# A graph layer and a routed expert layer on one core: four neighbouring tokens to a partition for x and the output, chunk 0 loaded behind x's first group, and the first chunks' projections one group ahead

## What is computed

```python
def reference(x, adj, ...):
    # graph layer, on the layer-normalised x
    h = layernorm(x)
    filt = tanh(adj * adj) * (adj > 0)
    new_adj = filt, with the 350 largest entries of each row kept
    h2 = tanh(h @ W_proj + b_proj)
    x = x + relu(new_adj @ (h2 @ W_gcn) + b_gcn)
    # expert layer, on the layer-normalised x
    t = layernorm(x)
    gate = t @ Wg.T + bg                  # (4096, 8)
    s, idx = top_k(gate, 2); p = softmax(s)
    for e in range(8):
        y = relu(t @ W1[e].T + b1[e]) @ W2[e].T + b2[e]
        x = x + combine[:, e] * y         # combine: p where e is in idx
    return x
```

## Time and profile before

| | us |
|---|---|
| median of 3 runs | 454.85 |
| lowest and highest | 454.68, 456.05 |
| profiled execution, its own time | 453.6 |
| its span, first to last instruction | 451.8 |
| PE busy | 399.7 (88%) |
| ACT busy | 329.6 (73%) |
| DVE busy | 324.6 (72%) |
| POOL busy | 201.3 (45%) |
| mean granted TensorE clock | 0.966 |

### The profile page before, as it was taken

One profiled execution on the slowest core, in us unless ns is written; L12 is line 12 of the kernel. 1 busy time (PEld: TensorE's weight loads), 2 busy tenths in 40 slices (PEclk: granted clock), 3 DMA queues, 4 the chain that ended last, 5 costly groups with the idle time before them and its releaser, 6 DMA issues.

```text
span 451.8 us, 7828 instructions
## 1 busy us (share of the span) xinstructions
PE 399.7 (88%) x2392; PEld 231.9 (51%) x2392; DVE 324.6 (72%) x946; ACT 329.6 (73%) x329; POOL 201.3 (45%) x296
## 2 busy tenths in 40 slices
PE   1799999999899899999999999999697999999600
PEld 1555434344344344444454544446596889999500
DVE  5977887562997898765849776964988766676435
ACT  2788999679989879979989989953454666666300
POOL 5048976000005303512610846623657777777700
PEclk9999999999999999999999999999898999999955
DMA  8828997866378676866873979924533464531069
GB/s 248 324 96 295 411 400 258 303 232 247 107 265 309 205 270 217 306 259 220 311 284 107 319 224 319 301 41 80 95 73 119 115 114 106 103 88 59 22 243 318
DMA packets 54260, 95.01 MB, mean 210 GB/s; under 512 B 34037, under 2 KB 41258, under 8 KB 46018
## 3 DMA queue, kind: packets, MB, share of 16 engines
q1 hardware_dynamic: 43584, 79.40, 52.9%
q0 software_dynamic: 5920, 12.78, 8.8%
q10 hardware_dynamic: 4706, 2.23, 1.7%
HBM read 77.90 MB, written 12.27 MB: 200 GB/s over the span
## 4 chain that ended last, share of the span: by engine, by line
PE 64%; DVE 18%; issue 5%; ACT 4%; DMA 4%; POOL 1%; ACTq 1%; SPq 1%; POOLq 0%; DVEq 0%
PE bank L1453 35%; PE bank L1581 6%; PE bank L1468 3%; PE bank L1555 3%; ACT tbuf L1193 3%; PE bank L1582 3%; PE bank L1557 3%; PE bank L1556 3%; DMA tbuf<-expert_rows 2%; PE bank L1424 2%; DVE stats L745 1%; PE bank L1408 1%; DVE tbuf L1100 1%; PE bank L1540 1%; DVE aug L738 1%
## 5 line engine op out<-in xcount | busy, mean ns | idle before, releaser
L1453 PE MATMUL bank<-tbuf,g_sb 128*128 128x512 f32 x512 | 234.4, 602 | 0.3 <-ACT tbuf L1197 0.3
L1453 PEld LDWEIGHTS bank<-tbuf,g_sb 128*128 128x128 f32 x512 | 93.0, 192 | 101.1 <-issue 99.8
L1193 ACT ACTIVATE tbuf<-abuf 128x2048 f32<-128x2048 f32 x64 | 121.5, 1898 | 7.8 <-DVE key L1077 4.2
L1197 ACT ACTIVATE tbuf<-tbuf 128x2048 f32<-128x2048 f32 x64 | 122.3, 1911 | 2.0
L691 POOL DMA_INDIRECT routed_rows<-aug,slots x64 | 74.0, 1157 | 102.9 <-DVE base L904 83.5
L705 POOL DMA_INDIRECT expert_rows<-abuf,xmeta x72 | 70.9, 985 | 27.2 <-issue 16.5
L918 DVE TENSOR_SCALAR marks<-abuf 128x2048 bf16<-128x2048 int32 x64 | 80.4, 1265 | 2.0 <-PE bank L1468 1.9
L1581 PE MATMUL bank<-w2hl,tbuf 128*128 x288 | 53.5, 279 | 5.8 <-DVE tbuf L1100 5.8
L1582 PE MATMUL bank<-w2hl,tbuf 128*128 x288 | 51.6, 224 | 0.0
L1100 DVE SCALAR_TENSOR_TENSOR tbuf<-bank,tbuf 128x512 f16<-128x512 f32 x72 | 46.7, 685 | 5.8 <-ACT tbuf L1294 5.3
L1302 ACT ACTIVATE abuf<-bank,xmeta 128x128 f32<-128x128 f32 x72 | 23.0, 365 | 38.2 <-PE bank L1582 38.2
(11 more groups left out here) (246 smaller groups left out, 420.5 us busy)
## 6 DMA issues: line engine op xcount, KB each, us to landing
abuf<-in_adj_tiles SPq DMA_DIRECT2D x64, 1024.0 KB, 5.7
wstage<-in_w POOLq DMA_DIRECT2D x16, 256.0 KB, 7.1
tbuf<-expert_rows SPq DMA_DIRECT2D x8, 512.0 KB, 7.2
out<-xres ACTq DMA_DIRECT2D x8, 256.0 KB, 6.3
routed_rows<-pad SPq DMA_DIRECT2D x9, 130.0 KB
expert_rows<-abuf,xmeta POOLq DMA_INDIRECT x72, 2.4
routed_rows<-aug,slots POOLq DMA_INDIRECT x64
abuf<-routed_rows SPq DMA_TRANSPOSE x40
```

The lines of the kernel that those rows point to most:

```text
L1193: act.activation(tbuf[:, n % NBUF, :, :], abuf[:, n % NBUF, :, :], ACT.Square).then_inc(s_sq, 1)
L1197: act.activation(tbuf[:, n % NBUF, :, :], tbuf[:, n % NBUF, :, :], ACT.Tanh).then_inc(s_t, 1)
L1453: last = pe.matmul(ps_feat[ib % 2][:, :], g_sb[:, c, :], tbuf[:, buf, cc, :], start=(c == 0), stop=(c == C - 1))
```

## The change

Six things change; line numbers are those of before.

1. `xres` holds four neighbouring tokens in each partition: group g, partition p and column group c now hold token g*512 + 4p + c. `load_x` and the output store read and write 2048 contiguous bytes for each partition and group where they had four runs of 512.
2. The transposed normalised x comes out of PE in the order (c, p). `turned_out` writes it to `xnorm_t` in the order (p, c), a step of four elements (16 bytes) between neighbouring elements of its write. From there the projections read as before, and `g_sb`, the adjacency and the counts keep their order.
3. `features_back` reads its stationary operand from `feat_t` with a step of four elements (16 bytes), where it read 128 contiguous columns.
4. SP issues x piece 0, chunk 0, x piece 1, chunk 1, x piece 2, chunk 2, where it issued x piece 0, x piece 1, chunk 0, x piece 2, chunk 1.
5. PE transposes group 1 in the middle of chunk 0, and projects group n + 1 in the middle of chunk n for n of 1 and more; it transposes group n + 2 behind chunk n. ACT follows in the same order, and squares chunk 0 ahead of the first transposed group.
6. All steps of WAT lie one later.

```diff
-    WAT = [1 + i for i in range(2 * NPC)]
+    WAT = [2 + i for i in range(2 * NPC)]
...
-                sp.dma_start(xres[:, c0:c1, :], x[c0 * P:c1 * P, :].rearrange("(c p) d -> p c d", p=P)
-                             ).then_inc(s_x[i], 16)
+                sp.dma_start(xres[:, c0:c1, :].rearrange("p (g c) d -> p g c d", c=CK),
+                             x[c0 * P:c1 * P, :].rearrange("(g p c) d -> p g c d", p=P, c=CK)).then_inc(s_x[i], 16)
 
             load_x(0)
-            load_x(1)
             for n in range(NCH):
...
                 sp.dma_start(abuf[:, n % NBUF, :, :], adj_tiles[n // NK, n % NK, :, :, :]).then_inc(s_a[n % NBUF], 16)
-                if n == 0:
-                    load_x(2)
+                if n < 2:
+                    load_x(n + 1)
...
                 act.wait_ge(s_tr, g + 1)
-                act.activation(xnorm_t[:, g * IW:(g + 1) * IW], [ps_x2, ps_xn][g % 2][:, :], ACT.Copy
+                act.activation(xnorm_t[:, g * IW:(g + 1) * IW].rearrange("d (p c) -> d c p", c=CK),
+                               [ps_x2, ps_xn][g % 2][:, :].rearrange("d (c p) -> d c p", c=CK), ACT.Copy
                                ).then_inc(s_trc, 1)
...
+            square_chunk(0)
             turned_out(0)
-            square_chunk(0)
+            tanh_chunk(0)
             projected_out(0)
-            tanh_chunk(0)
-            turned_out(1)
...
                     square_chunk(n + 1)
+                    if n == 0:
+                        turned_out(1)
                     tanh_chunk(n + 1)
-                if n == 0:
-                    projected_out(1)
-                    turned_out(2)
+                if n + 1 < NK:
+                    projected_out(n + 1)
                 if n + 2 < NK:
-                    projected_out(n + 2)
-                if n + 3 < NK:
-                    turned_out(n + 3)
+                    turned_out(n + 2)
...
-                act.dma_start(out[g * IW:(g + 1) * IW, :].rearrange("(c p) d -> p c d", p=P),
+                act.dma_start(out[g * IW:(g + 1) * IW, :].rearrange("(p c) d -> p c d", p=P),
...
             project(0)
-            turn_group(1)
...
                 for cc in range(SUB):
-                    c = b * SUB + cc
-                    last = pe.matmul(x2[:, cc * D:(cc + 1) * D], feat_t[:, c * P:(c + 1) * P], wg_sb[:, :],
+                    last = pe.matmul(x2[:, cc * D:(cc + 1) * D], feat_t[:, b * IW + cc:(b + 1) * IW:SUB], wg_sb[:, :],
...
                 for cc in range(CK):
+                    if n + 1 < NK and cc == CK // 2:
+                        project(n + 1) if n else turn_group(1)
...
                 if n == 0:
                     project(1)
-                    turn_group(2)
                 if n + 2 < NK:
-                    project(n + 2)
-                if n + 3 < NK:
-                    turn_group(n + 3)
+                    turn_group(n + 2)
```

More of the change, by code:

```diff
@@ L527, in _ @@
                 all_stored(NT)
-                sp.dma_start(xres[:, :, :], x.rearrange("(c p) d -> p c d", p=P)).then_inc(s_xre, 16)
+                sp.dma_start(xres[:, :, :].rearrange("p (g c) d -> p g c d", c=CK),
+                             x.rearrange("(g p c) d -> p g c d", p=P, c=CK)).then_inc(s_xre, 16)
                 sp.wait_ge(s_key, 1)
```

## The result

| | before | after |
|---|---|---|
| median, us | 455.38 (4 runs, 454.68 to 456.05) | 462.59 (4 runs, 462.07 to 463.3) |
| profiled execution, its own time / span | 453.6 / 451.8 | 462.9 / 461.2 |
| PE busy | 399.7 | 407.5 |
| ACT busy | 329.6 | 332.5 |

The ratio is 1.0169, 95% interval 1.0143 to 1.0194: between 6.5 and 8.8 us slower, 7.2 by the medians, where +5.1 was forecast. The profiled execution of before was a quick one of its kind, so the two traces differ by 9.4 us, about 2 more than the medians.

The account below looks back on a forecast made before the run. PE bounds 100 to 300 us; DVE, POOL and `s_one` fix the early counts at 33.6. 453.6 + 0.4 - 0.1 + 0.7 + 4.5 - 0.4 = 458.7 us profiled; from median 454.85, +5.1 gives 459.9, range 453.2 to 463.5.

Parts of the forecast that it names:

- The stationary operand in steps, +4.5: `features_back`: 56 stepped `feat_t` loads in PE's stream cost 80 ns more each, +4.5 us; bounds 0 and 6.7.
- one for one: PE between 100 and 300 us: any earlier or later arrival, or longer PE work, moves the end by the same amount.
- ACT's copies, +0.7: Start, chunks 4 to 7: stepped writes cost up to 0.48 us a copy, making ACT slower than PE; +0.7 us (0 to 2.0).
- The new order, +0.4: Start: PE's 2.5 us lead is lost waiting for `s_one`; one transposed group then stands behind the wait, +0.4 us.
- the cap: Counts of chunks 0 and 1: DVE, POOL and `s_one` fix their start at 33.6 us, whatever PE has done.
- WAT, 0: Weight pieces one step later: no PE step waits for DVE's marks, and `w1` parts move within PE-bound work; 0.
- The clock: Rival within free steps: PE's clock halves behind 2.9 us idle before the counts, costing 1.5 us, 456.2 us; chance 0.10.
- x and its order, -0.1 and 0: Start loads: piece 0 of x lands 0 to 0.4 us sooner, -0.1 us; piece 2 lands just in time, 0.
- the other end: Start: piece 2 of x lands late and stalls DVE 2.0 us; as a rival with free steps 456.7 us, chance 0.05.
- The output, -0.4: End: longer store runs save at most 1.6 us but may delay the last load; -0.4 us (-1.6 to +0.7).

Follow-up runs that it names:

- layout alone: Kernel before with only x and output four tokens to a partition, the copies' stepped write and the stepped stationary operand; old start order and WAT. Ratio 1.0112.
- the early semaphore: Changed kernel with POOL setting its constants and raising `s_one` ahead of its wait for the normalised groups and its weight loads. Ratio 1.0094.

## Why the prediction was right, and where it was not

The direction, the cause and the range (453.2 to 463.5) held. The sum of +5.1 stands against 7.2 in the medians, or 7.6 in the traces once the experts' scatter is taken out. What it lacks is, for the most part, 0.7 of the reads, 0.3 of WAT, 0.5 to 0.8 of the clock and 0.2 of the copies.

- **The stationary operand in steps, +4.5.** Right in kind, at 5.2 measured, and nearer than it deserved, by two errors of opposite sign. A load grew by 137 ns and not by 80, more than the 119 that I had called the upper bound from DVE's slope: the price of one engine was no bound for another's. Of that, 107 ns a load reached PE's time (1.91 against 1.05 for eight), 6.0 us in the stream. Then 0.8 were swallowed by PE's wait for the early rows' counts behind the first block, which I had not allowed for: "one for one" was wrong there. With the reads put in (layout alone) or taken out, the stretch changed by 5.2. Of the two readings of the Trainium skill ("SBUF — State Buffer"), the requirement of two hits on a line (Specifications) is the one that 192 to 329 and 592 to 1096 ns bear out; "4 fp32" as a free stride (Door 1) is wrong for these accesses if it is read as a step of four elements.
- **ACT's copies, +0.7.** Measured 0.9 at the experts' start. The copy rose by 504 ns where I had bounded it at 480. Right in size, as far as one trace tells. The mechanism stands on the waits: those for `g_sb` fell by 0.5 when the copies were contiguous.
- **The new order, +0.4, and the cap.** The step held. PE idled in front of the counts, released by POOL, the lead was lost, and the early semaphore removed the wait. That it idled 2.88 us, where I had 2.9, is luck: chunk 2 ended at 31.88 and not at 30.7, and the counts came at 34.76 and not at 33.6. With WAT put back it idled 2.17. The 0.4 for the transposed group was not measured by itself. What I had not weighed is that raising `s_one` early is worth 3.3 us to this kernel, where it is worth 0.5 to the kernel before.
- **WAT, 0.** This term failed. I asked whom DVE's marks keep waiting and looked at PE alone. They hold POOL's DMA issue, which stands on the chain I had just read: +1.13 us at the counts. It then gave 0.8 back in the stream, which I had not foreseen either, so the sum suffered by 0.3 only: luck again. The place to see it was the earlier trace rows: four issues of 3.70 us, of which one took 2.1 and ended with DVE's marks.
- **The clock.** I had it as a part of a rival, at 1.5 us. It fell in after and in three of the other kernels that had such a wait, but stayed at 1.00 in one with 2.8 us of idle. Filled, it gave 0.8 at chunk 8 and 0.5 at the experts. So it belonged into the forecast, at half a microsecond or a little more.
- **x and its order, -0.1 and 0.** Right: piece 0 landed 3.0 us after its issue (before 3.1) and piece 2 in time. The price of 2.0 for the other end was seen as well, with the old layout: waits of 1.85 and 0.71 us.
- **The output, -0.4.** Measured -0.3, in one pair of traces and in the means of nine and four kernels, by the two opposed effects that the term named: the last sum 1.6 us later, the last store 1.9 us quicker. The Trainium skill ("DMA: Bandwidth & Descriptors", Specifications) puts line rate at 512 B and above, by which the stores would not change; here the quickest landing went from 3.9 to 2.0 us and the longest issue from 2239 to 382 ns.

At the start the parts add up so: 1.2 (POOL's issues), 0.4 (the transposed group, as forecast), 0.8 (clock), 0.9 (copies) make 3.3 of the 3.6 us at chunk 8, within the scatter of a start. In the stream 5.2 (reads) less 0.8 (WAT) make the 4.3.

## What to carry over

When a layout change buys longer DMA runs, ask where the permutation goes: here a step of 16 bytes cost 137 ns a weight load and 504 ns a copy's write when it lay in SBUF, and nothing when it lay in PSUM, read by ACT or written by PE. Before letting an engine run ahead, read the chain of the wait it will meet, down to the queue of the engine that raises it; moving that raise up by a few lines was worth 3.3 us here, and the lead by itself nothing. An edit to one engine's order must be priced at every engine that it keeps from working, DMA issue of GpSimd included. And before a change in a wait is put down to one cause, compare the same stretch in every kernel that was traced: here that showed that half of the 1.6 us of lost waits were WAT's.

## What the hardware showed that I had not expected

- A step of 16 bytes made PE's load of 128 fp32 columns 1.7 times as long (192 to 329 ns), and ACT's write of 512 fp32 elements to SBUF 1.9 times (592 to 1096).
- In PSUM the same step was free: ACT's copy of 512 elements 580 ns with it and 580 without, PE's 128-column transposes 273 ns with it and 273 without. The Trainium skill ("SBUF — State Buffer", Door 1: The DMA port swizzle) says that any non-contiguous pattern in PSUM slows matmuls significantly. For these fp32 transposes the measurement says otherwise; a bf16 multiplication was not tried.
- POOL's first weight load issue took 2.1 us beside two marks of DVE and 3.2 beside three, and ended 0.1 us behind the last of them both times.
- The granted clock fell to 0.50 behind 2.88 and 2.17 us without PE work and stayed at 1.00 behind 2.81 us in another run, so the length of the idle stretch alone did not decide it.
